# Layer normalisation in one VectorE instruction: two per-partition scalar columns, or one column and a broadcast tensor operand

## The reference

```python
def _layernorm(x, axis=-1, eps=1e-05):
    m = jnp.mean(x, axis=axis, keepdims=True)
    v = jnp.var(x, axis=axis, keepdims=True)
    return (x - m) / jnp.sqrt(v + eps)
...
h = _L0_tok_ref(x, L0_tok_W)                        # embedding + positions
h = h + _L0_attn_ref(_layernorm(h, axis=-1), ...)   # group norm, 8 heads of 64, own residual
h = h + _L0_ffn_ref(_layernorm(h, axis=-1), ...)    # two masked 128x128 layers with gelu
h = h + _L1_attn_ref(_layernorm(h, axis=-1), ...)   # 8 heads of 16
h = h + _L1_ffn_ref(_layernorm(h, axis=-1), ...)    # 16 experts, top-1 routing with capacity
```

## Time and profile before

| | us |
|---|---|
| median of 3 runs | 6807.82 |
| lowest and highest | 6796.63, 6813.67 |
| the profiled execution | 6804.59 |
| its span in the profile | 6802.8 |
| TensorE matmul busy | 6049.1 (89%) |
| VectorE busy | 4474.2 (66%) |
| ScalarE busy | 3218.6 (47%) |
| GpSimd busy | 2516.2 (37%) |
| mean granted TensorE clock | 0.951 |

### The profile page before, as it was taken

The page is one execution under the profiler, slowest core; times in us unless marked ns, Lnnn a source line. Parts: engine busy times, 40 slices in busy tenths (PEclk is TensorE's granted clock), DMA queues, the critical chain, the costliest instruction groups (busy, mean ns, idle before and its releaser), DMA issues.

```text
span 6802.8 us, 126677 instructions
## 1 busy us (share of the span) xinstructions
PE 6049.1 (89%) x40167; PEld 4017.5 (59%) x40167; DVE 4474.2 (66%) x11034; ACT 3218.6 (47%) x6321; POOL 2516.2 (37%) x2135
## 2 busy tenths in 40 slices
PE   6788898998989889898998989989898998989986
PEld 4556665665656666565665656666565665656543
DVE  4456676776757667576776767767676676767664
ACT  2345545444444444554544444454544544454531
POOL 3534433433333333333433333343333433333300
PEclk7899999999999999999999999999999999999987
DMA  2121221221122121211212222121211212222110
GB/s 59 41 67 41 58 51 29 63 51 46 46 53 49 39 52 42 59 42 38 63 42 49 49 50 49 44 50 45 59 42 38 63 34 57 49 50 44 25 30 9
DMA packets 98046, 317.01 MB, mean 47 GB/s; under 512 B 27782, under 2 KB 32854, under 8 KB 87126
## 3 DMA queue, kind: packets, MB, share of 16 engines
q1 hardware_dynamic: 97366, 308.41, 19.6%
HBM read 57.19 MB, written 41.94 MB: 15 GB/s over the span
## 4 chain that ended last, share of the span: by engine, by line
issue 44%; POOL 25%; PE 22%; DVE 4%; ACT 2%; DMA 2%; SPq 1%; POOLq 1%; DVEq 0%; ACTq 0%
POOL pr_lo L506 21%; PE bank L884 4%; PE bank L912 3%; PE bank L945 3%; POOL on L1265 2%; PE bank L910 2%; PE bank L870 2%; PE bank L929 2%; PE bank L930 2%; DMA stacks<-parts 1%; DVE mxh L1630 1%; PE bank L719 1%; PE bank L818 1%; PE bank L708 1%; PE bank L955 1%
## 5 line engine op out<-in xcount | busy, mean ns | idle before, releaser
L1630 DVE TENSOR_REDUCE mxh<-bank 128x1 f32<-128x512 f32 x4096 | 2789.0, 688 | 1797.3 <-PE bank L884 1779.6
L1143 ACT ACTIVATE pr<-bank 128x512 f32<-128x512 f32 x4096 | 2418.4, 598 | 2723.7 <-PE bank L912 2679.9
L884 PE MATMUL bank<-stacks 128*128 128x512 f32 x4096 | 2221.3, 543 | 348.4 <-DVE mxh L1630 233.9
L506 POOL TENSOR_TENSOR pr_lo<-pr 128x1024 bf16<-128x1024 f32 x1024 | 1944.7, 1902 | 911.4 <-ACT pr L1143 909.1
L912 PE MATMUL bank<-stacks 65*128 65x512 f32 (+1 forms) x4096 | 1673.2, 409 | 27.7 <-ACT pr L1143 27.7
L884 PEld LDWEIGHTS bank<-stacks 128*128 128x128 f32 x4096 | 799.9, 195 | 1090.2 <-DVE mxh L1630 757.7
L929 PE MATMUL bank<-v,pr 128*128 128x129 bf16 x8192 | 1063.5, 222 | 94.6 <-POOL pr_lo L506 93.3
L930 PE MATMUL bank<-v,pr_lo 128*128 128x129 bf16 x8192 | 1051.1, 220 | 0.0
L929 PEld LDWEIGHTS bank<-v,pr 128*128 128x128 bf16 x8192 | 779.5, 98 | 393.1 <-issue 346.3
L1265 POOL TENSOR_TENSOR on<-on,o_r 128x128 f32<-128x128 f32 x512 | 205.4, 401 | 2045.5 <-DVE on L1660 2045.4
L912 PEld LDWEIGHTS bank<-stacks 65*128 65x128 f32 (+1 forms) x4096 | 800.2, 195 | 261.4 <-ACT pr L1143 94.4
(11 more groups left out here) (170 smaller groups left out, 4925.2 us busy)
## 6 DMA issues: line engine op xcount, KB each, us to landing
stacks<-parts SPq DMA_DIRECT2D x384, 512.0 KB, 6.5
stacks<-parts_d SPq DMA_DIRECT2D x224, 128.0 KB, 3.0
parts_d<-mx SPq DMA_DIRECT2D x16, 1024.0 KB, 4.5
stacks<-parts_d SPq DMA_DIRECT2D x224, 64.0 KB, 2.8
stage<-in_pe SPq DMA_DIRECT2D x16, 512.0 KB, 7.8
stacks<-mrow SPq DMA_DIRECT2D x512, 2.0 KB
parts_d<-on SPq DMA_DIRECT2D x16, 512.0 KB, 5.2
parts_d<-stage SPq DMA_DIRECT2D x16, 512.0 KB, 6.2
```

Source lines behind the costliest of these rows:

```text
L506: return eng.tensor_tensor(low_of(u, kt - 1).rearrange("p a b -> p (a b)"), w, hi, ALU.subtract)
L884: mm(maxb[k % 2][:, :], qs[:, t * P:(t + 1) * P], ks[:, g * HALF:(g + 1) * HALF], start=True, stop=True).then_inc(max_filled.sem, 1)
L1143: act.activation(pr[:, at % 2, kt, :], score[k % 2][:, :], ACT.Exp, scale=SCALES[layer]).then_inc(exp_done.sem, 1)
L1630: dve.tensor_reduce(mxh[:, layer, n // 2, n % 2:n % 2 + 1], maxb[k % 2][:, :], AX_X, ALU.max)\
```

## The change

The instruction of `norm_apply` took two [128 x 1] columns, the mean and the reciprocal root, as its two scalar operands. Now only the mean is a scalar column; the reciprocal root is read as a second tensor operand, the same column repeated over the 128 channels by a stride of zero. The arithmetic, the count of instructions, their order and all waits and signals are as before.

```diff
                         t = 4 * g + j
-                        ins = dve.tensor_scalar(dst[:, t, :], tokens[:, t, :], mv[:, s, t, 0:1], rs[:, s, t:t + 1],
-                                                ALU.subtract, ALU.mult)
+                        ins = dve.scalar_tensor_tensor(dst[:, t, :], tokens[:, t, :], mv[:, s, t, 0:1],
+                                                       rs[:, s, t:t + 1].broadcast_to([P, C]), ALU.subtract, ALU.mult)
                     ins.then_inc(z_ready[n].sem, 1)
```

## The result

Over 20 runs of each, the changed kernel takes 6817.9 us in the median (6806.4 to 6843.2) against 6807.6 (6794.9 to 6819.3). The ratio is 1.0019, with a 95% interval of 1.0011 to 1.0026: 7 to 18 us slower, or 0.19%. The forecast was 6815, or +7.8 us against the kernel before, within the 0.3% that was called no change. The profiled execution took 6816.3 us (span 6814.5).

A forecast was written before the change was run, and what follows sets the result against it. TensorE's matmuls fill 89% of the span, with VectorE's bursts holding TensorE up. Held tails 4.2, GpSimd's loss 1.7, free instructions on `stage` and `hm`, and 0.8 on `h` gave +7.8 us: median about 6815, range 6790 to 6845.

The forecast's parts named there:

- Step 1: In bursts on `stage` and `hm`, the new form is held beside GpSimd like the old: 0 of 94 us come back.
- rival of the free port: The new form isn't held beside GpSimd, so bursts on `stage` and `hm` shorten: median 6701 us; chance 0.07.
- Step 2: Each of 70 held instructions ends 0.06 us later behind GpSimd's instruction: 4.2 us.
- Step 3: GpSimd's second subtraction in each of 28 back-to-back pairs is delayed by 0 to 0.06 us: 1.7 us taken.
- Step 4: Where nothing holds it, the new form costs 0.006 us more from start to start: 2.6 us for 442 instructions.
- rival of the reading time: The second tensor costs 0.06 us on each of the 442 free instructions too: +32 us, median 6840; chance 0.03.
- The sum: Steps on `stage` and `hm` wholly, 7.0 us, plus half of the 1.5 us on `h`, 0.8: +7.8 us.
- Nothing else moves: Order, signals, transfers and other queues stay, and no further GpSimd instruction is caught behind a burst: no further term.
- on the path wholly: Added time in bursts on `stage` and `hm` counts in full, as TensorE waits right behind them: 7.0 us.
- The clock rival: TensorE's clock falls behind all 14 bursts on `hm` as idle time grows to 2.2 us: 22 us, median 6838; chance 0.10.
- The forecast's own range: Median of 6795 to 6835 us: 6808 to 6818 by the bounds, some 17 us either side for scatter.

The follow-up runs named there:

- experiment 1: A kernel without the computation, running only bursts of 8 VectorE instructions in eight forms, alone, beside reading subtractions or memsets: new form 344, 925, 343 ns.
- half of the change: New form only in the bursts on `stage` and `hm`, old form on `h`, against the kernel before: ratio 1.0018, or 12 us (5 to 19).
- The fillers: Old form kept, extra `bn_stats` ahead of the last instruction of bursts on `stage` and `hm`, against the kernel before: +11 us single dose, +47 fourfold in both.
- experiments 11 and 12: Old form with the fourfold `bn_stats` dose in bursts on `stage` alone, then on `hm` alone, against the kernel before: +10 and +30 us.

## Why the prediction was right

**Step 1, the new form is held: right.** It rested on L1593 and L1476 by analogy; the bursts after and experiment 1 show it directly, with 925 ns beside reading subtractions and 344 alone. The reason given, that what is held has two tensor operands in SBUF, was too narrow: the old form has one and was held too, and so are one column (864 ns) and the copy (827). The rival of the free port (0.07) is out for this GpSimd work. It would have been right for a neighbour that only writes.

**Step 2, the tail: right.** +0.06 us for each held instruction was taken; 0.15 in place of 0.09 us was seen in one, 0.148 in place of 0.082 in the medians. The bursts came out at 6.46 and 4.94 us; 6.4 and 4.95 were forecast.

**Step 3, GpSimd's loss: right, at the upper end too high.** 0.04 us for each pair of subtractions, 0.06 was taken.

**Step 4, the free form: right.** 0.263 against 0.257 us from start to start. The estimate from the Trainium skill, "VectorE: DVE Perf Modes", 0.067 us for the second tensor, is right for the tensor by itself (0.066 in experiment 1). As a forecast for the change it would have been wrong, since the column that goes, at 0.061 us, isn't in it. The rival of the reading time (0.03) is out: +12 us for half of the change lie in the held bursts, and 256 free instructions cost nothing that can be told.

**The sum: right in size, with one term missing, and in part by luck.** +7.8 us was the forecast, +10.4 in the medians and +13 by the ratio were measured, and 7.8 is just inside the interval (7 to 18). The term that is missing is the granted clock, which the sum put at nothing ("Nothing else moves") and gave to a rival alone. The fillers bear out "on the path wholly" on `stage`, with 10 us (4 to 16) for the 9.9 that arrived. On `hm` they don't: 9.4 us cost 30, and the mean clock was 0.0039 lower. For the change the split above gives the clock some 9 us, as much as all terms of the sum together. A forecast without that term stayed inside the interval because the interval is wide.

**The clock rival (0.10): right that the clock matters, wrong on how.** I asked whether all 14 bursts on `hm` would pass a point. Behind three of the 14 the clock was lower, behind one before, and no such point was found: 4 and 8 of 14 with the idle time as it was, 5 and 8 of 14 at 2.60 us. By the means the clock contributed perhaps 9 us where the rival priced it at 22. It should have stood in the sum as a share, beside the forecast, instead of as a case of its own.

The range (6790 to 6845) held the 6817.9 us. (The forecast's own range was added up wrongly at its lower end: 6808 less 17 is 6791, not 6795. Nothing hangs on it.) The change is slower by 0.19%: within the 0.3% that I called no change, though 20 runs tell it from zero.

## What to carry to other kernels

A long maximum beside a normal median in a VectorE line is worth a look at GpSimd's timeline: here all forms tried whose operands all lie in SBUF were held beside reading GpSimd instructions, and keeping the two apart gave 68 to 79 us, where the two forms differ by 13. Swapping one form for another pays only if the new one isn't held. Moving an operand to PSUM did that in experiment 1; one tensor less did not (the copy is held as well). Count every operand, as a scalar column (0.061 us) costs nearly as much as a second tensor of 128 elements (0.066). And a delay behind which TensorE idles needn't be worth its length: measure it with a filler at several doses and places, and look in the trace how much of the dose arrived. Here a part of one vanished beside a hold, and another cost three times its length while the granted clock fell.

## What the runs showed that was not expected

- The new form is not held by GpSimd instructions that only write SBUF (343 ns against 344, in experiment 1), though the old one is, as expected (739 against 341).
- 9.4 us of filler behind `hm` cost 30 us (21 to 39), and a dose of 16.5 us behind `stage` cost 10 (4 to 16). In the profile of the second only 9.9 us of it arrived. It also has the longer idle time, 5.5 us and more, and the clock behind it was at half already, so there may have been little left to lose; that is argued, not shown.
- Runs of one and the same kernel differ in their mean clock by 0.003 to 0.006, where there are 11 runs or more, and in time with it: 0.946 to 0.951 and 6794.7 to 6820.7 us for the kernel before, beside experiments 11 and 12. A single profiled execution can't carry a claim of 10 us about the clock: the kernel with the new form on `h` alone had 9 us more of matmul time in its profile (6058.0 against 6049.1) and the same median as the kernel before.
